# First attention: a new table of work-bank tasks, the value product in halves, and two copies on other engines

## The chip, the cores and the metric

The kernel runs on one core of one Trainium2 chip. The metric is the device time of one execution in microseconds. TensorE (PE) does matrix products and transposes, VectorE (DVE), ScalarE (ACT) and GpSimd (POOL) the rest, SyncE (SP) issues DMAs. Each engine takes its instructions in order; they wait for each other by semaphores.

## The reference, cut to what matters

Four layers in a row, each followed by a layer norm of input plus output: an attention, a feed-forward of four small stages, a linear attention, and a feed-forward of six blocks. Only the first attention is changed. It has 4 batches of 512 rows of 256 numbers and 16 heads of 16:

```python
qkv = jnp.einsum('bsh,hf->bsf', hidden_states, w_qkv) + b_qkv
qkv = qkv.reshape(B, S, NUM_HEADS, 3 * HEAD_DIM)
# q, k, v per head; the first 4 of 16 dimensions of q and k are rotated
scores = jnp.einsum('bhqd,bhkd->bhqk', q, k)
causal = jnp.tril(jnp.ones((S, S), dtype=bool))
scores = jnp.where(causal, scores, jnp.float32(-jnp.inf).astype(scores.dtype))
probs = jax.nn.softmax(scores, axis=-1)
attn = jnp.einsum('bhqk,bhkd->bhqd', probs, v)
attn = jnp.transpose(attn, (0, 2, 1, 3)).reshape(B, S, H)
return jnp.einsum('bsh,hf->bsf', attn, w_out) + b_out
```

## The kernel before

`attention0` runs all four batches. An *entry* is one batch: `entry(0, "first")`, a loop over the two middle ones (`"loop"`), `entry(3, "last")`. An entry has 8 *pairs* p of heads, a pair has 4 *slots* r, one for each tile of 128 rows; (p, r) names a slot. Every engine has its own `entry` that walks the same 32 slots, so the order on each engine is written out by hand.

In a slot TensorE does `max_pass` for the pair after next (two products q x k into banks 0 and 1, from which VectorE's `maximum` takes the row maxima), in slot 1 `max_rows` (a transpose of the negated maxima into the exchange bank; VectorE's `take_rows` copies it out and a DMA puts it into `qT`), a piece of the `value_pass`, the `score_pass` (two products k x q into one of the banks 2 to 4), and at most one task of the *work bank*. ScalarE's `exponentials` make `probs` from the scores, GpSimd's `select` zeroes what lies behind the diagonal. `J_ORDER` gives the tile that a slot works on: 512, 128, 384 and 256 columns in slots 0 to 3. The value product of a group q (two pairs, four heads) is done in the four slots of pair 2q + 2, one piece in each, before the slot's scores. Then ScalarE's `copy_outputs` (slot 3 of that pair) moves the sums out of bank 6, and in slot 2 of the next odd pair `transpose_outputs` puts them through the exchange bank, from where VectorE's `take_outputs` divides them.

The work bank (PSUM bank 5) holds one task at a time; the next may begin when the reader of the last has read it. The tasks, from the tables `UNIT_AT`, `PREVIOUS` and `AHEAD`:
- `project` (half of the heads u, tile t): six products make q, k and v of one tile and 8 heads; VectorE's `take_work` adds the bias into `qkv`. Then GpSimd's `rotate` (four instructions), ScalarE's `stack_high` (two: the parts of q and k rounded to fp32r), VectorE's `stack_low` (two subtractions: the rest).
- `stack`: four transposes of `k_stack` into the work bank, four of `q_stack` into the exchange bank. VectorE copies the first to `kT` (line 1028), ScalarE the second to `qT` (`copy_q`, line 759).
- `x_T`, `att_T`, `next_T` (c = 0, 1): four transposes of the next batch's input, the finished attention or the finished norm of the batch before. ScalarE's `high` copies the rounded part, then VectorE's `low`, one slot later in its order, subtracts for the rest, and frees the bank.
- `out` (0, 1): twelve products with the output weights; VectorE adds the residual. Behind `out` 1 comes the layer norm, its steps spread over the slots from (4, 0) on.

In an entry the second half's four tiles are projected and stacked in pairs 0 to 2, the next batch's first half in pairs 4 to 6; `att_T`, `x_T` and `out` stand in (2, 2) to (3, 3), `next_T` in (6, 2) and (6, 3). Pair 7 has no task. The exchange bank (PSUM bank 7) is used in turn by `max_rows`, `stack` and `transpose_outputs`; its readers count up `ex_read`, those of the work bank `v_work`.

Before the first entry the weights are split and the first half of batch 0 is projected and stacked; after the last the value product of its last group and the last output are done. Then the next part of the kernel (`prep`) starts and fetches its weights.

## Time and profile before

| | us |
|---|---|
| median of 3 runs | 1283.71 |
| lowest, highest | 1275.53, 1283.94 |
| the profiled execution's own time | 1284.08 |
| its span, first to last instruction | 1282.4 |
| mean granted TensorE clock over the span | 0.899 |

The rows come from the profiled execution, with times in us from the start of its span. A granted clock of 1.00 in a stretch is 2.4 GHz throughout, 0.50 is 1.2 GHz throughout; nothing between is granted, so a mean tells the shares. The busy time of TensorE counts weight loads apart (PEld), which overlap the products. The first attention ends at about 385 us of the span.

### The profile page before, as it was taken

What the parts mean: (1) busy time and instruction counts of PE and PEld (TensorE: products, weight loads), DVE (VectorE), ACT (ScalarE), POOL (GpSimd) and SP (SyncE); (2) the same over time, 40 slices, a digit from 0 to 9 for tenths busy, and PEclk for the clock granted to TensorE, in tenths of its full rate; (3) what the DMA queues carried; (4) which work ended last, traced back from release to release, by engine and by line L of the source; (5) the groups of instructions that cost most, each with busy time, mean ns of one, the idle gap of its engine ahead of it and who ended that gap; (6) DMA issues with size and microseconds to landing.
All of it is one profiled execution on the core that took longest, in us unless ns stands there. A gap on an engine that the chain in (4) does not pass through costs nothing. (4 is left out here: it accounts for less than half of the span.)

```text
span 1282.4 us, 20711 instructions
## 1 busy us (share of the span) xinstructions
PE 1098.8 (86%) x6653; PEld 898.6 (70%) x6653; DVE 806.2 (63%) x2286; ACT 604.6 (47%) x1149; POOL 273.8 (21%) x361
## 2 busy tenths in 40 slices
PE   3789889889857667863886999999999999999996
PEld 3545455545435557863775898989989989989895
DVE  2666676577636257787357557666666676576664
ACT  2245534445422364534432746556466465564560
POOL 1223323134220230020001112312313214213200
PEclk9978887788778778975896999999999999999999
DMA  4000000000007100000001200101000000101110
GB/s 158 17 2 18 2 18 18 1 17 2 18 1 264 66 1 1 0 0 3 0 18 36 80 1 34 34 1 33 33 0 33 33 0 33 33 0 33 33 34 33
DMA packets 28589, 36.56 MB, mean 29 GB/s; under 512 B 1412, under 2 KB 25704, under 8 KB 28520
## 3 DMA queue, kind: packets, MB, share of 16 engines
q1 hardware_dynamic: 25912, 31.80, 7.4%
q10 hardware_dynamic: 2608, 3.93, 0.9%
q8 instruction: 33, 0.54, 0.2%
q14 instruction: 36, 0.29, 0.1%
HBM read 31.40 MB, written 4.19 MB: 28 GB/s over the span
## 5 line engine op out<-in xcount | busy, mean ns | idle before, releaser
L1825 ACT ACTIVATE G<-ps,bias_col 128x512 f32<-128x512 f32 x192 | 135.2, 704 | 188.8 <-PE ps L1743 177.5
L1758 PE MATMUL ps<-w_h,G_h 128*128 128x256 f32 x768 | 217.7, 283 | 1.4 <-DVE rsum L1886 1.4
L1758 PE MATMUL ps<-w_h,G_l 128*128 128x256 f32 x768 | 217.3, 283 | 0.0
L1758 PE MATMUL ps<-w_l,G_h 128*128 128x256 f32 x768 | 217.1, 283 | 0.0
L1877 DVE TENSOR_TENSOR G_l<-G,G_h 128x512 fp32r<-128x512 f32 x192 | 136.2, 719 | 62.9 <-ACT G_h L1826 62.8
L766 ACT ACTIVATE probs<-ps 128x512 f32<-128x512 f32 (+3 forms) x256 | 97.4, 436 | 148.5 <-PE ps L829 148.4
L1743 PE MATMUL ps<-xT_h,w_h 128*128 128x512 f32 x384 | 154.2, 401 | 1.7 <-PEq L1358 1.7
L1743 PE MATMUL ps<-xT_l,w_h 128*128 128x512 f32 x384 | 152.8, 398 | 0.0
L1743 PE MATMUL ps<-xT_h,w_l 128*128 128x512 f32 x384 | 152.6, 397 | 0.0
L1705 POOL TENSOR_TENSOR x_a<-xn,mlp_g 128x1024 f32<-128x1024 f32 x20 | 72.1, 3606 | 368.4 <-DVE xn L1909 368.4
L967 DVE CUSTOM_DVE_ANT_0 ps<-ps,q_mask 128x128 f32<-128x128 f32 (+3 forms) x256 | 121.5, 512 | 46.3 <-PE ps L818 39.6
L1758 PEld LDWEIGHTS ps<-w_h,G_h 128*128 128x128 f32 x768 | 147.2, 192 | 2.4 <-issue 1.6
L1758 PEld LDWEIGHTS ps<-w_l,G_h 128*128 128x128 f32 x768 | 147.2, 192 | 0.8
L1758 PEld LDWEIGHTS ps<-w_h,G_l 128*128 128x128 f32 x768 | 147.2, 192 | 0.0
L1826 ACT ACTIVATE G_h<-ps,bias_col 128x512 fp32r<-128x512 f32 x192 | 134.7, 702 | 0.0
L1886 DVE TENSOR_TENSOR rsum<-ps,x_a 128x1024 f32<-128x1024 f32 x24 | 29.4, 1224 | 118.7 <-PE ps L1758 118.7
L680 POOL TENSOR_SCALAR_AFFINE_SELECT probs<-probs 128x256 f32<-128x256 f32 x128 | 52.0, 409 | 209.1 <-ACT probs L766 209.0
L818 PE MATMUL ps<-kT,qT 64*128 64x128 f32 (+3 forms) x256 | 77.5, 475 | 19.5 <-DVE top_score L967 18.9
L1743 PEld LDWEIGHTS ps<-xT_h,w_h 128*128 128x128 f32 x384 | 72.9, 190 | 18.5 <-issue 2.0
L1871 DVE TENSOR_TENSOR xT_l<-hs,xT_h 128x512 fp32r<-128x512 f32 x40 | 80.5, 2039 | 7.8 <-ACT xT_h L1813 7.7
L1743 PEld LDWEIGHTS ps<-xT_h,w_l 128*128 128x128 f32 x384 | 72.9, 190 | 17.4
L1743 PEld LDWEIGHTS ps<-xT_l,w_h 128*128 128x128 f32 x384 | 73.0, 190 | 16.6
(248 smaller groups left out, 2165.1 us busy)
## 6 DMA issues: line engine op xcount, KB each, us to landing
w_raw<-L_ffn_W_T SPq DMA_DIRECT2D x12, 1024.0 KB, 5.1
hs<-L_attn_hidden_states SPq DMA_DIRECT2D x8, 512.0 KB, 3.5
x_kept<-hs SPq DMA_DIRECT2D x4, 512.0 KB, 2.9
w_raw<-x_kept SPq DMA_DIRECT2D x2, 1024.0 KB, 5.9
out<-xn SPq DMA_DIRECT2D x4, 512.0 KB, 2.9
w_raw<-L_ffn_ent_w_T SPq DMA_DIRECT2D x1, 1024.0 KB, 10.5
w_raw<-L_ffn_ent_pw SPq DMA_DIRECT2D x1, 1024.0 KB, 12.6
qT<-neg_rows SPq DMA_DIRECT2D x64, 2.0 KB
```

The costliest lines, as they stand in the source:

```text
L680: pool.affine_select(diagonal, diagonal, [[0, 2], [1, P]], ALU.is_ge, 0.0, base=0, channel_multiplier=-1).then_inc(s["g_sel"], 1)
L766: act.activation(probs[:, p % 2, o, OFF[j]:OFF[j] + COLS[j]], ps[:, score_bank(r, o), 0:COLS[j]], ACT.Exp).then_inc(s["a_exp"], 1)
L818: pe.matmul(ps[:, o, 0:(t + 1) * P], qT[rows, p, t * P:(t + 1) * P], kT[rows, p, 0:(t + 1) * P], start=True, stop=True).then_inc(s["p_max" ...
L967: v.tensor_tensor_reduce(ps[:, o, 0:(t + 1) * P], ps[:, o, 0:(t + 1) * P], q_mask[:, S - (t + 1) * P:S], 1.0, MASKED, ALU.add, ALU.max, to ...
L1705: pool.tensor_tensor(g.x_a[:, rows, :], xn[:, b % 2, :, :], bcast(g.mlp_g[:, i, :], 1, [P, RT, D]), ALU.mult).then_inc(s["g_mul"], 1)
L1743: mm = pe.matmul(ps[:, n % 4, :], w[:, c, f * P:(f + 1) * P], x[:, b, c, :], start=(k == 0), stop=(k == 5))
L1758: mm = pe.matmul(ps[:, 4 + t // 2, (t % 2) * D:(t % 2 + 1) * D], x[:, b % 2, f, t * P:(t + 1) * P], w[:, f, :], start=(k == 0), stop=(k == ...
L1825: act.activation(G32[:, n % 4, :], ps[:, n % 4, :], ACT.Gelu, bias=bias)
L1826: act.activation(G_h[:, b % 2, f, :], ps[:, n % 4, :], ACT.Gelu, bias=bias).then_inc(s["a_g"], 1)
L1871: v.tensor_tensor(g.xT_l[:, b, c, :], src, g.xT_h[:, b, c, :].bitcast(F32), ALU.subtract).then_inc(s["v_T"], 1)
L1877: v.tensor_tensor(G_l[:, b % 2, f, :], G32[:, n % 4, :], G_h[:, b % 2, f, :].bitcast(F32), ALU.subtract).then_inc(s["v_gl"], 1)
L1886: v.tensor_tensor(g.rsum[:, :, :], ps[:, 4:6, :].rearrange("p a (b c) -> p (a b) c", c=D), g.x_a[:, b * RT:(b + 1) * RT, :], ALU.add).then ...
```

## The change

One table `WORK_AT` takes the place of three and spreads the tasks over all eight pairs. Heads are counted in halves: 1 is the second half of the batch, 2 and 3 are both halves of the next. The second half of the next batch is now projected in pairs 6 and 7 of the entry before it, and only stacked in its own; in the preparation its four projections stand between the first maxima. The slots of `stack_high` and of the low parts are given by `HIGH_AT` and `LOW_AT`. `stack_low` moves from VectorE to GpSimd, the copy of `kT` from VectorE to ScalarE (`copy_k`, ahead of `copy_q`). The scores stand before the value product in a slot; the value product of group q is done in slots 2 and 3 of pair 2q + 1 and slots 0 and 1 of pair 2q + 2; `copy_outputs` comes in slot 2, `transpose_outputs` and `take_outputs` in slot 3 of that same pair. `v_work` is renamed `work_read`, `v_stack` `g_stack`. The diff, cut:

```diff
-UNIT_AT = ((0, 0, "project", 0), (0, 2, "project", 1), (0, 3, "stack", 0), (1, 0, "project", 2),
-           (1, 1, "stack", 1), (1, 2, "project", 3), (1, 3, "stack", 2), (2, 1, "stack", 3))
-VALUES_AT = {(1, 0): (0, 1), (1, 1): (2,), (1, 3): (3,)}
-PREVIOUS = ((2, 2, "att_T", 0), (2, 3, "att_T", 1), (3, 2, "out", 0), (3, 3, "out", 1),
-            (6, 2, "next_T", 0), (6, 3, "next_T", 1))
-AHEAD = ((3, 0, "x_T", 0), (3, 1, "x_T", 1))
+
+
+WORK_AT = ((0, 0, "stack", (1, 0)), (0, 2, "stack", (1, 1)), (0, 3, "x_T", 0),
+           (1, 0, "stack", (1, 2)), (1, 1, "x_T", 1), (1, 3, "stack", (1, 3)),
+           (2, 0, "att_T", 0), (2, 1, "project", (2, 0)), (2, 2, "att_T", 1),
+           (3, 0, "out", 0), (3, 1, "project", (2, 1)), (3, 3, "out", 1),
+           (4, 0, "stack", (2, 0)), (4, 1, "project", (2, 2)), (4, 2, "stack", (2, 1)),
+           (5, 0, "project", (2, 3)), (5, 1, "stack", (2, 2)), (5, 3, "stack", (2, 3)),
+           (6, 0, "project", (3, 0)), (6, 1, "project", (3, 1)), (6, 2, "next_T", 0),
+           (7, 0, "project", (3, 2)), (7, 1, "next_T", 1), (7, 3, "project", (3, 3)))
+HIGH_AT = {(0, 0): (1, 1), (0, 2): (1, 2), (1, 1): (1, 3), (3, 2): (2, 0), (4, 0): (2, 1), (4, 3): (2, 2),
+           (5, 2): (2, 3), (7, 2): (3, 0)}
+LOW_AT = {(0, 1): (1, 1), (0, 3): (1, 2), (1, 2): (1, 3), (3, 3): (2, 0), (4, 1): (2, 1), (5, 0): (2, 2),
+          (5, 3): (2, 3), (7, 3): (3, 0)}
+VALUES_AT = {(0, 3): ((1, 0), (1, 1)), (1, 0): ((1, 2),), (1, 1): ((1, 3),),
+             (4, 3): ((2, 0), (2, 1)), (5, 0): ((2, 2),), (5, 2): ((2, 3),)}
+PREVIOUS = ("att_T", "out", "next_T")
+AFTER = [(kind, n) for kind in PREVIOUS for n in range(2)]
+BEFORE = [("project", (2, 0)), ("project", (2, 1)), ("stack", (2, 0)), ("project", (2, 2)),
+          ("stack", (2, 1)), ("project", (2, 3)), ("stack", (2, 2)), ("stack", (2, 3))]
+
+
+def of_entry(when, half):
+    return half == 1 or when != "last"
 
 
 def work_table(when):
 
-    rows = [(p, r, kind, (1, t)) for p, r, kind, t in UNIT_AT]
-    if when != "last":
-        rows += [(p + 4, r, kind, (0, t)) for p, r, kind, t in UNIT_AT] + list(AHEAD)
-    if when != "first":
-        rows += PREVIOUS
-    return {(p, r): (kind, arg) for p, r, kind, arg in sorted(rows, key=lambda row: row[:2])}
+    table = {}
+    for p, r, kind, arg in WORK_AT:
+        if kind in PREVIOUS:
+            used = when != "first"
+        else:
+            used = when != "last" if kind == "x_T" else of_entry(when, arg[0])
+        if used:
+            table[p, r] = (kind, arg)
+    return table
+
+
+def group_at(p, r, when):
+    return r == RT - 1 and p % 2 == 0 and (p > 0 or when != "first")
 
...
                 uses.append((kind, arg))
-            if r == 2 and p % 2 and (p > 1 or when != "first"):
-                uses.append(("group", (p - 3) // 2))
+            if group_at(p, r, when):
+                uses.append(("group", p // 2 - 1))
...
+            def stack_low(i, half, t):
+                pool.wait_ge(s["a_stack"], tile_number(i, half, t) + 1)
+                heads = qkv[:, t, :].rearrange("p (h c d) -> p h c d", h=UH, c=3)
+                pool.tensor_tensor(q_stack[:, :, DH:2 * DH], heads[:, :, 0, :],
+                                q_stack[:, :, 0:DH].bitcast(F32), ALU.subtract)
+                pool.tensor_tensor(k_stack[:, :, 2 * DH:3 * DH], heads[:, :, 1, :],
+                                k_stack[:, :, 0:DH].bitcast(F32), ALU.subtract).then_inc(s["g_stack"], 1)
...
+                        if (p, r) in LOW_AT and of_entry(when, LOW_AT[p, r][0]):
+                            stack_low(i, *LOW_AT[p, r])
                         select(i, p, r)
                         kind, arg = table.get((p, r), (None, None))
                         if kind == "project":
                             rotate(i, when, *arg)
-                        u = 1 if p < UP else 0
-                        if (p % UP, r) in VALUES_AT and (u or when != "last"):
-                            if (p % UP, r) == (1, 0):
-                                wait(pool, s["p_out"], i * GROUPS + (0 if u else GROUPS // 2))
-                                pool.sem_inc(g.carrier["g_carrier"], 1)
-                            for t in VALUES_AT[p % UP, r]:
-                                values(i, u, t)
+                        for half, t in VALUES_AT.get((p, r), ()):
+                            if of_entry(when, half):
+                                if t == 0:
+                                    wait(pool, s["p_out"], i * GROUPS + (half - 1) * GROUPS // 2)
+                                    pool.sem_inc(g.carrier["g_carrier"], 1)
...
             for t in range(RT):
-                rotate(-1, "before", 0, t)
-                values(-1, 0, t)
+                rotate(-1, "before", 2, t)
+                values(2, t)
+                stack_low(-1, 2, t)
+            for t in range(RT):
+                rotate(-1, "before", 3, t)
+            stack_low(-1, 3, 0)
...
+            def copy_k(i, when, half, t):
+                u = half % 2
+                act.wait_ge(s["p_work"], WORK.number(i, when, ("stack", (half, t))))
+                act.activation(kT[:, u * UP:(u + 1) * UP, t * P:(t + 1) * P],
+                               work.rearrange("p (b c) -> p b c", c=P), ACT.Copy).then_inc(s["work_read"], 1)
+
+            def copy_q(i, when, half, t):
+                u = half % 2
+                act.wait_ge(s["p_ex"], EXCHANGE.number(i, when, ("stack", (half, t))))
                 act.activation(qT[:, u * UP:(u + 1) * UP, t * P:(t + 1) * P],
                                exchange.rearrange("p (b c) -> p b c", c=P), ACT.Copy).then_inc(s["ex_read"], 1)
...
                         exponentials(i, p, r)
-                        if r == RT - 1 and p % 2 == 0 and (p or when != "first"):
+                        if r == 2 and p % 2 == 0 and (p or when != "first"):
                             copy_outputs(i, when, p // 2 - 1, ("neg", p + 1))
                         kind, arg = table.get((p, r), (None, None))
                         if kind == "stack":
+                            copy_k(i, when, *arg)
                             copy_q(i, when, *arg)
                         elif kind in ("x_T", "att_T", "next_T"):
                             high(i, when, kind, arg)
-                        if before[0] == "project":
-                            stack_high(i, *before[1])
-                        before = (kind, arg)
+                        if (p, r) in HIGH_AT and of_entry(when, HIGH_AT[p, r][0]):
...
-                        if p and p % 2 == 0:
-                            value_pass(i, p // 2 - 1, r)
-                        elif p == 0 and when != "first":
-                            value_pass(i - 1, GROUPS - 1, r)
                         score_pass(i, p, r)
+
+                        if p % 2 and r >= 2:
+                            value_pass(i, p // 2, r - 2)
+                        elif p % 2 == 0 and r < 2 and p:
+                            value_pass(i, p // 2 - 1, r + 2)
+                        elif p == 0 and r < 2 and when != "first":
+                            value_pass(i - 1, GROUPS - 1, r + 2)
                         if (p, r) in table:
                             use_work(i, when, *table[p, r])
-                        if r == 2 and p % 2 and (p > 1 or when != "first"):
-                            transpose_outputs(i, when, (p - 3) // 2)
+                        if group_at(p, r, when):
+                            transpose_outputs(i, when, p // 2 - 1)
...
-            for _, _, kind, t in UNIT_AT:
-                use_work(-1, "before", kind, (0, t))
+            for kind, arg in BEFORE:
+                use_work(-1, "before", kind, arg)
             for p in range(2):
                 for t in range(RT):
                     max_pass(0, p, t, (-1, "before"))
+                    if p == 0:
+                        use_work(-1, "before", "project", (3, t))
                     if p and t == 1:
                         max_rows(-1, "before", 0, 0)
             entries(pe, entry)
-            for r in range(RT):
+            for r in range(2, RT):
                 value_pass(B - 1, GROUPS - 1, r)
             transpose_outputs(B - 1, "after", GROUPS - 1)
-            for _, _, kind, arg in PREVIOUS:
+            for kind, arg in AFTER:
                 use_work(B, "after", kind, arg)
 
...
-            def stack_low(i, u, t):
-                v.wait_ge(s["a_stack"], tile_number(i, u, t) + 1)
-                heads = qkv[:, t, :].rearrange("p (h c d) -> p h c d", h=UH, c=3)
-                v.tensor_tensor(q_stack[:, :, DH:2 * DH], heads[:, :, 0, :],
-                                q_stack[:, :, 0:DH].bitcast(F32), ALU.subtract)
-                v.tensor_tensor(k_stack[:, :, 2 * DH:3 * DH], heads[:, :, 1, :],
-                                k_stack[:, :, 0:DH].bitcast(F32), ALU.subtract).then_inc(s["v_stack"], 1)
 
...
-                elif kind == "stack":
-                    u, t = arg
-                    v.tensor_copy(kT[:, u * UP:(u + 1) * UP, t * P:(t + 1) * P],
-                                  work.rearrange("p (b c) -> p b c", c=P)).then_inc(s["v_work"], 1)
...
-                    kind, arg = table.get(slots[n - 2], (None, None)) if n >= 2 else (None, None)
-                    if kind == "project":
-                        stack_low(i, *arg)
                     kind, arg = table.get((p, r), (None, None))
-                    if kind in ("project", "stack", "out"):
+                    if kind in ("project", "out"):
                         take_work(i, when, kind, arg)
-                    if r == 2 and p % 2 and (p > 1 or when != "first"):
-                        take_outputs(i, when, (p - 3) // 2)
```

## Rows read from the trace of the kernel before

**Rows 1.** The page: busy time by engine, the clock by slices, two groups of section 5.
```profile
span 1282.4 us, 20711 instructions
...
PE 1098.8 (86%) x6653; PEld 898.6 (70%) x6653; DVE 806.2 (63%) x2286; ACT 604.6 (47%) x1149; POOL 273.8 (21%) x361
...
PEclk9978887788778778975896999999999999999999
...
L766 ACT ACTIVATE probs<-ps 128x512 f32<-128x512 f32 (+3 forms) x256 | 97.4, 436 | 148.5 <-PE ps L829 148.4
...
L818 PE MATMUL ps<-kT,qT 64*128 64x128 f32 (+3 forms) x256 | 77.5, 475 | 19.5 <-DVE top_score L967 18.9
```
**Rows 2.** Windows: busy us (instructions) by engine; clock; preparation, four entries, tail.
```profile
0.00:52.16 52.16, 24.94 (x84) 17.49 (x84) 20.48 (x60) 9.42 (x17) 8.60 (x26) 1.00 0.30 101
52.16:124.62 72.46, 66.25 (x373) 39.03 (x373) 49.54 (x189) 35.87 (x93) 22.77 (x72) 0.85 0.05 13
124.62:208.22 83.60, 70.68 (x445) 43.32 (x442) 56.49 (x209) 38.83 (x98) 25.91 (x74) 0.85 0.04 14
208.22:296.83 88.61, 75.73 (x444) 46.01 (x441) 57.92 (x217) 38.62 (x98) 25.94 (x74) 0.77 0.02 7
296.83:361.00 64.17, 58.20 (x353) 33.20 (x349) 40.39 (x156) 32.36 (x82) 18.32 (x52) 0.79 0.03 10
361.00:385.00 24.00, 12.51 (x74) 7.76 (x72) 8.50 (x28) 2.53 (x6) 3.83 (x4) 0.71 0.00 1
```
**Rows 3.** Windows of the second entry, same columns: about pair 2, pair 3, pair 7.
```profile
141.00:151.50 10.50, 8.44 (x71) 4.30 (x71) 7.70 (x28) 5.94 (x16) 2.51 (x7) 1.00 0.01 4
151.50:167.20 15.70, 11.76 (x65) 8.13 (x65) 8.34 (x29) 4.75 (x11) 1.64 (x4) 0.67 0.01 1
...
199.10:208.20 9.10, 7.66 (x31) 3.54 (x31) 5.55 (x21) 3.55 (x9) 4.84 (x6) 0.62 0.18 61
```
**Rows 4.** Timeline of the second entry, x_T 0 and 1 in the work bank.
```profile
153.15 0.84 PE L898 MATMUL ps<-ident,hs 128*128 128x128 f32 x4 [1.19 <-DVE att_l L1004]
...
154.02 0.60 ACT L741 ACTIVATE x_h<-ps 128x512 fp32r<-128x512 f32 x1 [0.94 <-PE ps L898]
...
155.62 0.67 DVE L1004 TENSOR_TENSOR x_l<-ps,x_h 128x512 fp32r<-128x512 f32 x1
...
156.34 1.12 PE L898 MATMUL ps<-ident,hs 128*128 128x128 f32 x4 [1.14 <-DVE x_l L1004]
```
**Rows 5.** Timeline of the second entry, the norm's statistics and TensorE's next product.
```profile
169.59 1.40 DVE L95 BATCH_NORM_STATS2 ln_stats<-rsum 128x6 f32<-128x256 f32 x4
...
172.37 0.82 PE L818 MATMUL ps<-kT,qT 64*128 64x384 f32 x2 [2.33 <-DVE top_score L967]
```
**Rows 6.** Groups by line and shape, 44 to 362 us; the number before the second bar: mean ns.
```profile
L1028 DVE CAST kT<-ps 128x512 fp32r<-128x512 f32 x28 | 19.1, 683 | 1.4 <-PE ps L876 1.4
...
L759 ACT ACTIVATE qT<-ps 128x512 fp32r<-128x512 f32 x28 | 16.8, 602 | 13.2 <-PE ps L903 13.2
...
L754 ACT ACTIVATE k_stack<-qkv 128x256 fp32r<-128x256 f32 x28 | 11.6, 413 | 0.0
...
L1013 DVE TENSOR_TENSOR k_stack<-qkv,k_stack 128x128 fp32r<-128x128 f32 x28 | 7.9, 283 | 0.0
```
**Rows 7.** Groups of GpSimd by line and shape, the whole span.
```profile
L691 POOL TENSOR_TENSOR hs<-hs,b_out 128x1024 f32<-128x1024 f32 x4 | 9.4, 2358 | 0.0
L665 POOL TENSOR_TENSOR turned<-qkv,rope 128x64 f32<-128x64 f32 x32 | 9.4, 294 | 47.2 <-DVE qkv L1024 47.0
...
L672 POOL COPY val<-qkv 128x128 f32<-128x128 f32 x32 | 9.0, 293 | 0.0
```
**Rows 8.** Timeline of the preparation: a projection's reader, a stack, the first maxima.
```profile
28.50 0.56 DVE L1024 TENSOR_TENSOR qkv<-ps,b_qkv 128x384 f32<-128x384 f32 x1 [2.38 <-PE ps L869]
...
34.79 0.72 PE L876 MATMUL ps<-ident_r,k_stack 128*128 128x128 f32 x4 [1.26 <-DVE k_stack L1013]
...
39.54 0.47 PE L818 MATMUL ps<-kT,qT 64*128 64x128 f32 x2
```

More of the change, by code:

```diff
@@ L512, in number @@
         return (i - 1) * len(self.lists["loop"]) + start + self.lists[when].index(key) + 1
-WORK = Uses([("x_T", 0), ("x_T", 1)] + [(kind, (0, t)) for _, _, kind, t in UNIT_AT],
-            lambda when: list(work_table(when).values()), [row[2:] for row in PREVIOUS])
-EXCHANGE = Uses([("stack", (0, t)) for t in range(RT)] + [("neg", 0)], exchange_list, [("group", -1)])
+WORK = Uses([("x_T", 0), ("x_T", 1)] + BEFORE + [("project", (3, t)) for t in range(RT)],
+            lambda when: list(work_table(when).values()), AFTER)
+EXCHANGE = Uses([("stack", (2, t)) for t in range(RT)] + [("neg", 0)], exchange_list, [("group", -1)])
 def attention0(nc, A, g):
@@ L776, in entry @@
                 table = work_table(when)
-                before = (None, None)
                 for p in range(PAIRS):
@@ L794, in _ @@
             for t in range(RT):
-                stack_high(-1, 0, t)
-                copy_q(-1, "before", 0, t)
+                stack_high(-1, 2, t)
+                copy_k(-1, "before", 2, t)
+                copy_q(-1, "before", 2, t)
+            stack_high(-1, 3, 0)
             entries(act, entry)
@@ L1089, in _ @@
                             ALU.subtract).then_inc(s["wsplit_l"], 1)
-            for n, (_, _, kind, t) in enumerate(UNIT_AT):
-                if kind == "stack":
-                    stack_low(-1, 0, t)
-                take_work(-1, "before", kind, (0, t))
+            for kind, arg in BEFORE:
+                if kind == "project":
+                    take_work(-1, "before", kind, arg)
             for p in range(2):
@@ L1096, in _ @@
                     maximum(0, p, t)
+                    if p == 0:
+                        take_work(-1, "before", "project", (3, t))
                     if p and t == 1:
```

57 lines of the change are left out of this document (30 added, 27 removed).

## Prediction

> **What bounds the kernel now.** I read the page first. TensorE is busy 86% of the span, the other engines 63% or less, and the row of granted clock sinks to 5 to 8 tenths in the first third of the span [rows 1]. The chain that ended last cannot be followed back past 703 us, so for the stage that is changed I read the windows by stage instead. The four entries of the batch loop last 72.46, 83.60, 88.61 and 64.17 us; before them lie 52.16 us of preparation, after them 24 us of tail [rows 2]. In the entries TensorE is busy 270.86 of 308.84 us, 88%, while VectorE has about 66%, ScalarE under 50%, GpSimd 30%. TensorE is nearly the bound, and two things make it long. It stands idle for 308.84 - 270.86 = 38.0 us. And its clock is below full: a granted mean c means that a share 2(1 - c) of the stretch ran at 1.2 GHz, which is 0.30, 0.30, 0.46 and 0.42 of the four entries, 21.7 + 25.1 + 40.8 + 27.0 = 114.6 us. What is busy there would take half the time at 2.4 GHz: 114.6 x 0.88 / 2 = 50 us. So entries with the same work would need about 308.8 - 38.0 - 50 = 221 us if nothing waited and the clock stayed up. The gain to be had is large, and most of it is clock.
>
> Next I asked where the clock falls. The stretch of pair 2, stacks, transposes and value product together, keeps 2.4 GHz although TensorE is idle for 2 of its 10.5 us; pair 3, with no value product, has 0.67; pair 7, with no task and no value product, 0.62 [rows 3]. The lulls are where the work is thin. In pair 3 the timeline shows why TensorE also stands still: transposes into the work bank (0.84 us), ScalarE copies the high part (0.60), VectorE, behind its maxima, makes the low part (0.67), and only then may TensorE use the bank again, after 1.14 us idle [rows 4]. In a middle entry five uses of the bank stand behind such a user in the very next slot (att_T twice, x_T twice, next_T once): about 5 x 1.3 = 6.5 us. A different wait is the layer norm: its statistics keep VectorE for 1.40 us and hold the next maximum, TensorE waits 2.33 us [rows 5].
>
> **The change, part by part.** *The clock.* The tables move no work out of an entry as a whole (the loop still has 16 project and stack tasks and 8 others), but the projections, before in pairs 0, 1, 4 and 5, now stand in pairs 2 to 7, and each value product is cut in two halves, slots 2 and 3 of the odd pair and slots 0 and 1 of the next even one. No pair is left without a value product, and pairs 3 and 7, the thin ones of [rows 3], get projections. What is left thin is pairs 0 and 1, which lose theirs and hold four stacks and two transposes; pair 2 of before, of that sort, kept its clock, the start of pair 3 did not, so I let each entry keep about 12 us at 1.2 GHz, the length of those two pairs less their value halves: 48 us instead of 114.6. Gain (114.6 - 48) x 0.88 / 2 = 29 us. Bounds: nothing at all if the lulls only move, and 42 us if 5 us are left in each entry.
>
> *The bank's chain.* Of the five adjacent uses of a middle entry two remain (x_T 0 before a stack, att_T 0 before a project): 3 x 1.3 = 3.9 us less, twice. The last entry loses all its three, 3.9 us; the first has one before and after. Sum 12 us.
>
> *VectorE.* It loses per full entry 8 copies of kT at 0.683 us and 16 subtractions at 0.285 [rows 6]: 5.5 + 4.6 = 10 us of some 57 busy. It is not the bound, so only its waits count: TensorE's score products of the maxima waited 18.9 us for it in all [rows 1], of which some 7 belong to the norm, that stays. I take 5 of the rest as gained; ends 0 and 12.
>
> *ScalarE.* It gets the kT copy, at the price of its neighbour qT, 0.602 us [rows 6]: 8 x 0.60 = 4.8 us an entry onto 38.8 busy. Before, VectorE copied kT while ScalarE copied qT. Now one engine does exponentials, kT, qT, and in three slots the two stack_high copies of 0.41 as well. Behind qT waits the exchange bank. After the new tables max_rows (slot 1) comes right after the stacks of (0,0), (1,0) and (4,0), and transpose_outputs right after that of (4,2), which on ScalarE also stands behind copy_outputs. From the end of the k transposes the copies need 0.60 + 0.60, and TensorE has about 0.35 us of other work to cover them: 0.85 us idle, three times; for (4,2) 1.2 us. That is 3.75 us in three entries, 1.7 in the last, and 2 in all for the kT copy that holds the work bank where the exponentials come late: 15 us more. Ends: 7 (ScalarE is early) and 56 (below).
>
> *GpSimd.* No row shows its subtraction of 128x128. From 128x64 at 0.294 us and 128x1024 at 2.358 [rows 7] the slope is 2.15 ns an element, so 0.43 us, two of them 0.87 a tile instead of VectorE's 0.57. Ends 0.29 (its own copy of that size, one input) and 0.6. Per entry 7 us on an engine with 26 busy; HIGH_AT and LOW_AT leave at least one slot of about 2 us for it before the transposes. Only from (4,0) to (4,2) is the chain full (kT, qT, two stack_high, two subtractions, 2.9 us, against some 3.5 us of TensorE's work), so I cost it at nothing; without that cover it would be 0.3 us a tile, 9 us in all. The Trainium skill speaks against this part: GPSIMD Engine Reference, § 4.1, gives two-input elementwise work to VectorE, as GpSimd is about 2x slower there. By it a tile costs twice 0.57, 1.14 us, an estimate 0.27 us over mine and still under the cover, so the sum would be the same; the page's rule counts an engine's time, and here GpSimd's time is idle. The rows for the same work (0.43 extrapolated against 0.285) say 1.5x.
>
> *Scores before values.* The exponentials start sooner by one piece of the value product; ScalarE is not the bound, I cost it at nothing. The value product needs select two slots back instead of four: two exponentials of 0.44 us on average [rows 1] and select end inside one slot.
>
> *Preparation.* Four projections (3, t) come into it, one behind each max_pass of pair 0, from 39.54 us on, where VectorE set the pace. Each is 2.38 us there, with VectorE waiting [rows 8]; half is hidden: +4 us. The low parts no longer stand behind the next take_work on VectorE (1.26 us of TensorE's wait in each tile, [rows 8]), about 0.7 us sooner in three tiles: -2. The same four leave the last entry; that is inside its shares. *Tail.* Two of four value passes leave the 24 us tail: -2.
>
> Sum: -29 (clock) - 12 - 5 + 15 (idle, together -2) + 4 - 2 - 2 = -31 us. The stage's end moves everything behind it, since the next weights are fetched when it ends. The profiled execution took 1284.08 us (span 1282.4), 0.4 over the median of 1283.71: 1284 - 31 = 1253.
>
> **The rivals.** *More than that:* the clock stays up everywhere but 5 us an entry (-42) and new waits are 7 instead of 15 (-8 more): 1253 - 13 - 8 = 1232. For it: pair 2 of before at 1.00. Against it: thin pairs 0 and 1.
>
> *The lulls only move:* the new waits and thin pairs 0 and 1 take back what pairs 3 and 7 give; 114.6 us stay at 1.2 GHz. Then only idle and ends count: 1284 - 2 = 1282, no change. For it: pair 3 of before fell to 1.2 GHz with gaps of little over 1 us [rows 3, 4].
>
> *ScalarE becomes the bound, slower:* each of the 28 stack slots in the entries shows its whole chain of 0.60 + 0.60 + 0.82 = 2.0 us on TensorE: 56 us instead of 15, that is 1253 + 41 = 1294. Place: max_rows and transpose_outputs behind the stack. It decides from 31 / 28 = 1.1 us a stack more than I took. Against it: pairs 0 and 1, the densest for ScalarE, ask of it 16 exponentials at 0.436 us [rows 1], four stacks at 1.20, three stack_high at 0.82, two x_T and one out_T at 0.60: 16.1 us, while two pairs of a middle entry take 20.9.
>
> **How the numbers follow.** The forecast 0.52 (own range 1240 to 1266), more 0.22, lulls only move 0.16, ScalarE bound 0.08, the rest anything. Over 1% is what a measurement of this kernel can tell from no change, 12.8 us, so below 1271 is faster: 0.52 + 0.22 + 0.03 = 0.77; 0.14 same; 0.09 slower. The range takes in the larger gain and most of the case without change: 1228 to 1284, leaving out some 0.17.
>
> **What would show it.** Right: the clock of the entries at 0.90 or more on average, with the rest of the low clock in pairs 0 and 1; pair 3 near 12 us instead of 15.7; idle of the entries near 35 us; TensorE's wait for VectorE's maxima shorter; a new wait of max_rows and transpose_outputs for ScalarE's qT of about 0.85 us; GpSimd's subtraction at 0.4 to 0.5 us with nobody waiting. Wrong: a clock at 0.81 or less as before; ScalarE leading the releasers of TensorE's waits with over 40 us; GpSimd's low parts released late to the k transposes.

## The result and the profile after

| | before | after |
|---|---|---|
| median, us | 1282.4 | 1241.26 |
| lowest, highest | 1275.53, 1283.94 | 1239.62, 1246.83 |
| span of the profiled execution | 1282.4 | 1237.7 |
| end of the first attention in the span | 387.4 | 349.3 |

The medians are 41.1 us apart. The ratio, which goes by all runs of both kernels, is 0.9702, 95% interval 0.9666 to 0.9737: about 38 us of 1280. The profiled execution of the changed kernel is the fastest of its four and has the highest granted clock of them, 0.927 over the span against 0.916 to 0.920. The page of the changed kernel, the rows that answer to [rows 1]:

```profile
span 1237.7 us, 20729 instructions
...
PE 1068.4 (86%) x6653; PEld 876.2 (71%) x6653; DVE 773.8 (63%) x2190; ACT 619.8 (50%) x1181; POOL 300.8 (24%) x425
...
PEclk9879999998787889858998999999999999999998
...
L812 ACT ACTIVATE probs<-ps 128x512 f32<-128x512 f32 (+3 forms) x256 | 98.2, 437 | 113.0 <-PE ps L877 112.3
...
L866 PE MATMUL ps<-kT,qT 64*128 64x128 f32 (+3 forms) x256 | 78.3, 457 | 12.5 <-DVE top_score L1019 12.0
```

TensorE has the same 86% and the same 6653 products, in 30 us less of busy time. The windows by stage show where, as [rows 2] did: preparation, four entries, the start of the tail; columns as there.

```profile
0.00:54.48 54.48, 31.06 (x108) 22.89 (x108) 16.98 (x52) 12.19 (x23) 16.77 (x52) 0.96 0.29 98
54.48:123.03 68.55, 61.49 (x382) 36.52 (x383) 40.91 (x160) 40.00 (x101) 28.45 (x84) 0.83 0.03 10
123.03:193.84 70.81, 64.54 (x442) 38.05 (x442) 49.55 (x190) 42.66 (x106) 30.96 (x87) 0.95 0.05 17
193.84:266.74 72.90, 65.12 (x443) 38.65 (x444) 50.04 (x190) 42.78 (x106) 32.59 (x91) 0.95 0.04 11
266.74:324.00 57.26, 50.21 (x325) 26.09 (x325) 36.50 (x146) 33.61 (x84) 19.80 (x51) 0.85 0.04 11
324.00:350.00 26.00, 12.47 (x74) 8.18 (x70) 8.77 (x28) 3.64 (x7) 3.40 (x3) 0.70 0.00 0
```

Read them as the prediction read [rows 2]. The entries last 269.52 us instead of 308.84, 39.3 less. TensorE is idle for 269.52 - 241.36 = 28.2 us instead of 38.0. At 1.2 GHz it ran for 0.34 x 68.55 + 0.10 x 70.81 + 0.10 x 72.90 + 0.30 x 57.26 = 54.9 us. The view gives 114.6 us for before, but that is too little: its record of the clock begins only at 61.3 us of the span, and the view counts what is not recorded as full clock. The same product takes 0.52 us before that point and 0.34 behind it:

```profile
59.70 0.52 PE L869 MATMUL ps<-wqkv_h,x_l 128*128 128x384 f32 x1
...
64.12 0.34 PE L869 MATMUL ps<-wqkv_h,x_l 128*128 128x384 f32 x1
```

So the 9.1 us from 52.16 to 61.3 were at 1.2 GHz as well, which makes 123.7 us. The kernel e8 below, the same up to there, has this stretch on record at 0.50 and needs the same 10.54 us for pair 0 of the first entry. The preparation's 1.00 in [rows 2] and its 0.96 here are too high for the same reason; the record of the changed kernel begins at 47.0, so its entries are complete. With the busy share of 0.90 the low clock cost 24.6 us; before, with 0.877, it cost 54.2. So the 39.3 us are 29.7 of clock and 9.8 of idle time, and nothing is left over. Around them: the preparation is 2.3 us longer (54.48 against 52.16), the tail, up to the last transposes of the attention, 1.1 shorter (from 324.00 to 349.3 against 361.00 to 387.4). Together 38.1 us.

The rest of the span is 888.4 us after the attention, 895.0 in the profile of before. These 6.6 us are not the change's: the twelve variants below have 886.6 to 892.7 us there, among them e4, e7 and e8, which keep the old table (888.7, 890.0, 889.5).

Pairs 3 and 7 of the second entry, the thin ones of [rows 3]:

```profile
149.93:158.72 8.79, 8.79 (x64) 5.93 (x66) 6.31 (x24) 3.67 (x10) 3.44 (x11) 1.00 0.01 2
...
186.42:193.84 7.42, 7.42 (x50) 4.59 (x52) 6.34 (x24) 4.16 (x11) 5.07 (x10) 1.00 0.14 44
```

Pair 3 took 15.64 us slot by slot and takes 8.79, pair 7 9.08 and 7.42, without a moment of idle time and at full clock. What stood still where is in TensorE's waits in the entries (total us, times, longest): first before, 52 to 361 us of its span,

```profile
PE ps L818 <- DVE top_score L967: 15.3, 32, 2.3
PE ps L898 <- DVE att_l L1004: 6.3, 5, 1.3
PE ps L898 <- DVE x_l L1004: 3.7, 3, 1.4
PE ps L903 <- DVE neg_rows L981: 3.5, 7, 0.9
PE ps L883 <- DVE x_l L1004: 3.2, 2, 1.6
PE ps L898 <- DVE xT_l L1004: 3.2, 3, 1.3
```

then after, 54 to 324 us:

```profile
PE ps L866 <- DVE top_score L1019: 10.3, 25, 1.8
PE ps L900 <- ACT qT L805: 5.0, 10, 0.6
PE ps L923 <- DVE x_l L1056: 2.9, 3, 1.1
...
PE ps L917 <- DVE att_l L1056: 1.6, 2, 0.8
PE ps L906 <- ACT qT L805: 1.4, 2, 0.7
PE ps L950 <- DVE neg_rows L1033: 1.3, 3, 0.5
...
PE ps L923 <- POOL k_stack L714: 0.7, 2, 0.5
```

The bank's chain (att_l, x_l, xT_l) went from 16.4 to 4.5 us, the maxima from 15.3 to 10.3, and the new waits for ScalarE's qT are 6.4 us.

### The profile page after: what moved, and what is told of

It reads as the page before. It is cut to its first block and busy times, and to the rows that moved or that the text cites. A ratio compares the mean times of both kernels' runs of the same rounds, so it can differ in the third digit from the quotient of the medians.

```text
span 1237.7 us, 20729 instructions
## 1 busy us (share of the span) xinstructions
PE 1068.4 (86%) x6653; PEld 876.2 (71%) x6653; DVE 773.8 (63%) x2190; ACT 619.8 (50%) x1181; POOL 300.8 (24%) x425
## 5 line engine op out<-in xcount | busy, mean ns | idle before, releaser
L812 ACT ACTIVATE probs<-ps 128x512 f32<-128x512 f32 (+3 forms) x256 | 98.2, 437 | 113.0 <-PE ps L877 112.3
L866 PEld LDWEIGHTS ps<-kT,qT 64*128 64x128 f32 x256 | 37.3, 204 | 63.1 <-DVE top_score L1019 45.8
```

Of the source, the lines that this page charges most:

```text
L812: act.activation(probs[:, p % 2, o, OFF[j]:OFF[j] + COLS[j]], ps[:, score_bank(r, o), 0:COLS[j]], ACT.Exp).then_inc(s["a_exp"], 1)
L866: pe.matmul(ps[:, o, 0:(t + 1) * P], qT[rows, p, t * P:(t + 1) * P], kT[rows, p, 0:(t + 1) * P], start=True, stop=True).then_inc(s["p_max" ...
```

## The experiments

The prediction put most of the gain on the filling of thin pairs, by the table and by the halves of the value product, and nothing on the order of scores and values. The rival theory is a chain: scores, exponentials, the rounded parts of a stack (ScalarE), its low parts, then the stack's transposes on TensorE. By it, what makes the chain late makes TensorE stand still for a microsecond, and the clock falls soon after; then every part of the change that shortens the chain is worth more than its own time. The table has all kernels that ran. Ratios are to before, run beside each variant on the same chip, with medians of 1280.34 us (e3 to e6), 1279.56 (e7 to e10) and 1277.29 (e1, e2, e11, e12); so compare the ratios, not the medians.

Idle and low clock are us of the four entries, from windows as above; for before, e4 and e7 the first 9.1, 9.7 and 9.8 us, which are not on record, are counted as low. The last column counts TensorE's standstills of over 1.0 us that begin at full clock in the entries. These three columns come from one profiled execution each, and executions differ: the mean granted clock of 57 executions of before was 0.885 to 0.910, and the two middle entries of the one profiled, with the same instructions, had 25.1 and 40.8 us of low clock. A difference of some 15 us in that column can be chance.

| kernel | median us | ratio, interval | idle | low clock | over 1.0 |
|---|---|---|---|---|---|
| before | 1282.4 | 1 | 38.0 | 123.7 | 10 |
| after | 1241.26 | 0.9702, 0.9666 to 0.9737 | 28.2 | 54.9 | 3 |
| e4 before + both engine moves | 1275.66 | 0.9977, 0.9942 to 1.0012 | 37.9 | 126.9 | 9 |
| e7 before + halves behind the scores | 1280.14 | 1.0006, 0.9974 to 1.0038 | 37.6 | 123.9 | 8 |
| e8 before + scores twice, pairs 3, 7 | 1277.54 | 1.0003, 0.9964 to 1.0043 | 35.0 | 99.1 | 10 |
| e3 after, both engine moves undone | 1256.88 | 0.9827, 0.9764 to 0.9890 | 30.7 | 85.1 | 5 |
| e1 after, low parts on VectorE | 1251.76 | 0.9827, 0.9781 to 0.9873 | 31.0 | 82.2 | 5 |
| e2 after, kT copy on VectorE | 1248.51 | 0.9781, 0.9758 to 0.9803 | 25.1 | 75.2 | 2 |
| e5 after, values before scores | 1269.89 | 0.9919, 0.9890 to 0.9949 | 32.6 | 101.1 | 9 |
| e11 the same, only in one slot | 1269.64 | 0.9949, 0.9918 to 0.9980 | 33.5 | 97.2 | 4 |
| e6 after, values whole | 1272.92 | 0.9940, 0.9898 to 0.9983 | | | |
| e9 after + scores twice, pairs 1, 5 | 1244.02 | 0.9728, 0.9679 to 0.9777 | 24.6 | 59.8 | 1 |
| e10 after + fuller preparation | 1244.71 | 0.9722, 0.9674 to 0.9769 | 26.3 | 75.7 | |
| e12 after, another table | 1254.74 | 0.9843, 0.9805 to 0.9881 | 29.9 | 69.1 | 3 |

**e3, the table and the order without the engine moves.**

```diff
-            def stack_low(i, half, t):
-                pool.wait_ge(s["a_stack"], tile_number(i, half, t) + 1)
...
-                            copy_k(i, when, *arg)
...
+            def stack_low(i, half, t):
+                v.wait_ge(s["a_stack"], tile_number(i, half, t) + 1)
...
+                elif kind == "stack":
+                    half, t = arg
+                    u = half % 2
+                    v.tensor_copy(kT[:, u * UP:(u + 1) * UP, t * P:(t + 1) * P],
+                                  work.rearrange("p (b c) -> p b c", c=P)).then_inc(s["work_read"], 1)
```

> The changed kernel with VectorE again copying kT and making the low parts of the stacked heads; task table, halves of the value product and their order stay. Theory A (the gain is the even work on TensorE, which keeps its clock and breaks up the bank's chain; the engines matter little): about 1248 us, 7 over the changed kernel's 1241, entries' clock at 0.90 or more. Theory B (the gain is the 10 us of VectorE's work an entry that others took over): about 1275, with TensorE waiting for VectorE's maxima as before, 18 us or more.

1256.88 us: the table, halves and order are worth 22 us (0.0173 of 1280), the engine moves 16 more on top of them (7 to 25 with both intervals). Neither guess had come near: the time lies between 1248 and 1275, and TensorE waits 11.4 us for the maxima, not 18.

**e4, the engine moves alone, on the kernel before.** The same functions on ScalarE and GpSimd, in the slots that before has.

> The kernel before with only the engines changed: ScalarE copies kT, GpSimd makes the low parts; old tables, whole value product. Theory A: 1275 to 1285 us, entries' clock near 0.81 as before. Theory B: 1255 or less.

Nothing that can be told from no change; the profile has the same idle time and low clock as before, and a preparation 2.4 us shorter. So the two moves are worth 3 us (at most 7) on the old table and 16 on the new one. A price for them alone does not exist.

**e7, the halves behind the scores, on the kernel before.** The edit cuts the value product in halves and also puts the scores before it, so it tests the two together. It also takes the one-slot shift of copy, transposes and division that goes with them.

```diff
-                        if p and p % 2 == 0:
-                            value_pass(i, p // 2 - 1, r)
...
                         score_pass(i, p, r)
+                        if p % 2 and r >= 2:
+                            value_pass(i, p // 2, r - 2)
+                        elif p % 2 == 0 and r < 2 and p:
+                            value_pass(i, p // 2 - 1, r + 2)
```

> The kernel before (old task tables, old engines) with only the value product in two halves behind the scores, its copy and transposes one slot earlier. Theory A (what counts is how evenly TensorE is loaded, slot by slot): pairs 3 and 7 are no longer without a value product, their granted clock rises from 0.67 and 0.62, and the time falls by 10 to 20 us to 1260 to 1270. Theory B (the task table alone did it): within 5 us of the kernel before.

No change. Pair 3 of the second entry goes from 15.6 to 13.8 us, but the low clock of the entries stays, 123.9 against 123.7 us: in the middle entries there is less of it in pairs 0 and 3 and more in pairs 4 and 5. Giving the thin pairs half a value product, with the scores first, is worth nothing on the old table and the old engines.

**e8, more work in the thin pairs, on the kernel before.** Every score product of pairs 3 and 7 is done twice, into the same place.

```diff
+                    for n in range(2 if p in (3, 7) else 1):
+                        mm = pe.matmul(ps[:, score_bank(r, o), 0:COLS[j]], kT[rows, p, j * P:(j + 1) * P],
+                                       qT[rows, p, j * P:S], start=True, stop=True)
+                    mm.then_inc(s["p_score"], 1)
```

> The kernel before with both score products of every slot of pairs 3 and 7 done twice (the second writes the same result): 1.2 us more TensorE work a pair, 9.6 us in all, and no wait changed. Theory A (the clock falls in these pairs because TensorE has little to do in them, and that costs more than waits): granted clock there well above 0.67 and 0.62, time no longer than before, 1270 to 1283, in spite of the added work. Theory C (the clock falls because of the gaps): clock as before, time up by 5 to 10 us, 1286 to 1292.

The 9.6 us that were expected to be added are too much. By the rows a doubled slot at full clock lasts 0.11 to 0.30 us longer, which makes 5 to 7 us in all. The interval of the ratio reaches from 5 us less to 5.5 us more, so whether the added work cost anything is open. In the profile the pairs 3 and 7 have 36.5 us of low clock instead of 59.4, as the first theory had it, while pairs 0 and 1 of the first entry have 21.3 instead of 9.1, where the edit changes nothing. So thin stretches seem to matter, but filling them brought no gain. The standstills stay at 10.

**e5, the order undone, on the kernel after.**

```diff
-                        score_pass(i, p, r)
-
                         if p % 2 and r >= 2:
                             value_pass(i, p // 2, r - 2)
...
+                        score_pass(i, p, r)
```

> The changed kernel with the piece of the value product before the scores in each slot, as in the kernel before. As costed in the prediction (the order is worth nothing, ScalarE is not the bound): within 3 us of 1241. Rival (ScalarE, which now copies kT too, is starved by scores that come late): 1250 or more, with ScalarE's idle before the exponentials longer than in the changed kernel.

This costs 28 us (22 to 34 with both intervals), more than any other part taken out of the changed kernel, by an edit that changes no instruction, only which comes first. My costing at nothing was wrong and the rival right: over the span ScalarE waits 135.6 us for the scores instead of 112.3. The timeline of the changed kernel in slot (5, 2) of the second entry, from the max products on (start, duration, engine, what):

```profile
172.64 0.44 PE L866 MATMUL ps<-kT,qT 64*128 64x384 f32 x2
...
172.92 0.34 PE L877 MATMUL ps<-qT,kT 64*128 64x384 f32 x2
173.19 1.90 PE L890 MATMUL ps<-probs,val 128*32 128x512 f32 x8
173.29 0.87 ACT L812 ACTIVATE probs<-ps 128x384 f32<-128x384 f32 x2
...
174.36 0.42 ACT L793 ACTIVATE k_stack<-qkv 128x256 fp32r<-128x256 f32 x1
...
175.35 0.46 POOL L714 TENSOR_TENSOR k_stack<-qkv,k_stack 128x128 fp32r<-128x128 f32 x1
...
176.54 0.58 PE L923 MATMUL ps<-ident_r,k_stack 128*128 128x128 f32 x4
```

and of e5, the same slot:

```profile
179.66 0.44 PE L866 MATMUL ps<-kT,qT 64*128 64x384 f32 x2
...
180.03 1.07 PE L890 MATMUL ps<-probs,val 128*32 128x512 f32 x8
...
181.03 0.44 PE L877 MATMUL ps<-qT,kT 64*128 64x384 f32 x2
...
181.50 0.87 ACT L812 ACTIVATE probs<-ps 128x384 f32<-128x384 f32 x2 [1.14 <-PE ps L877]
...
182.56 0.42 ACT L793 ACTIVATE k_stack<-qkv 128x256 fp32r<-128x256 f32 x1
...
183.56 0.45 POOL L714 TENSOR_TENSOR k_stack<-qkv,k_stack 128x128 fp32r<-128x128 f32 x1
...
184.07 0.54 PE L923 MATMUL ps<-ident_r,k_stack 128*128 128x128 f32 x4 [1.13 <-POOL k_stack L714]
```

Counted from the max products, the scores begin at 0.28 us after, at 1.37 in e5; the exponentials at 0.65 and 1.84; the low part ends at 3.17 and 4.35. The whole chain is 1.2 us later, about the value piece's length (1.07 us), and TensorE stands 1.13 us before the stack. This pair of rows is no clean comparison, though. The changed kernel runs the slot at 1.2 GHz, where the same piece takes 1.90 us and covers more of the chain. And the low clock in these two pairs is equal: the changed kernel has 3.4 us of it in pair 5, e5 has 3.4 us in pair 6. Only in the third entry does e5 have more, 17.0 us against 3.4.

**e11, the order undone in one slot only.** This tells whether that place carries the loss.

```diff
+                        if p % 2 and r == 2:
+                            value_pass(i, p // 2, 0)
                         score_pass(i, p, r)
...
-                        if p % 2 and r >= 2:
+                        if p % 2 and r == 3:
```

> The changed kernel, but at the third slot of an odd pair, where the value piece is two 256-column halves long (512 columns), the piece stands before the score matmuls again; at the fourth slot it stays behind them. If the 28.6 us that the piece before the scores cost came mainly from this one place (late scores, late exponentials, a stack that waits over 1 us at (5,3), then low clock in pair 6), then most of it is lost here too: 1258 to 1270 us, the stack at (5,3) waits over 1 us, the low clock of the four entries adds up to over 85 us. If the loss was spread over both slots of every odd pair, about half of it or less: 1248 to 1256 us, low clock 60 to 80 us.

All of the loss is there: ratio 0.9949, e5 0.9919, the intervals overlap. The stack at (5, 3) of the first entry gives the clean comparison, at full clock in both; first the changed kernel, then e11:

```profile
106.38 0.51 PE L923 MATMUL ps<-ident_r,k_stack 128*128 128x128 f32 x4 [0.52 <-POOL k_stack L714]
```

```profile
108.33 0.51 PE L923 MATMUL ps<-ident_r,k_stack 128*128 128x128 f32 x4 [1.37 <-POOL k_stack L714]
```

In e11 the clock falls 0.5 us later, and pairs 6 and 7 have 20.9 us of low clock; in the changed kernel they have none. In e5 the same stack waits 1.51 us, and no fall follows. The row at (5, 3) of e11's second entry and its windows of pairs 5 and 6:

```profile
192.97 0.54 PE L923 MATMUL ps<-ident_r,k_stack 128*128 128x128 f32 x4 [1.27 <-POOL k_stack L714]
```

```profile
182.73:193.96 11.23, 9.12 (x58) 4.87 (x58) 7.84 (x30) 5.16 (x14) 5.13 (x16) 0.85 0.01 3
193.96:204.19 10.23, 9.73 (x56) 5.67 (x56) 5.29 (x20) 4.60 (x12) 3.54 (x12) 0.83 0.00 1
```

The changed kernel needs 9.55 and 8.76 us for these two pairs, at 0.82 and 1.00. With the longest piece of the value product in front (512 columns, slot 2 of the odd pairs) the scores are late where a stack hangs on them. The edit is in the third slot of all odd pairs; that the stack at (5, 3) alone carries the loss is not shown.

**e6, the value product in one pair.** On the kernel after: four pieces in the slots of the next even pair, before the scores, and copy_outputs, transpose_outputs and take_outputs where before had them.

> The changed kernel with each value product whole in the even pair, before the scores, as in the kernel before; task table and engines as changed. Theory A1 (the task table alone keeps TensorE's clock): within 6 us of 1241. Theory A2 (the halves are needed, since odd pairs without a value product are thin whatever their tasks): 1255 to 1265, with the granted clock below 0.8 in pairs 1, 5 and 7.

1272.92 us, by the ratio 0.9940 some 30 us over the changed kernel, near e5 and over both guesses. Halving the product gains nothing without the order: e5, halved and values first, is as slow. A whole product behind the scores was not tried. Only the times of e6 are used.

**e1 and e2, the engine moves one by one.** e1: stack_low as in the diff of e3; e2: the kT copy as there.

> The changed kernel, with the low parts of the stacked heads on VectorE again (the keys' copy stays with ScalarE). VectorE gets 10 tiles of 2 subtractions an entry back, 0.57 us a tile, and the stack no longer passes through GpSimd. If the 15.6 us that both moves give on top of the new table are VectorE's relief in proportion to the time taken from it (0.57 of about 1.4 us a tile), this loses about 6 us: 1247 us (1243 to 1252). If the chain ScalarE, then the low parts, then the stack decides, the faster engine for the low parts shortens it and the kernel is no slower than the changed one: 1238 to 1243 us.

> The changed kernel, with the copy of the transposed keys on VectorE again (the low parts stay on GpSimd). VectorE gets 10 copies an entry back, about 0.8 us each, in front of the transposed-query work and the row maxima; ScalarE gives up 0.60 us each. In proportion to VectorE's relief this loses about 9 us: 1250 us (1246 to 1256). If ScalarE's 0.60 us in front of an exponential cost as much as VectorE's copy did, there is no change: 1238 to 1244 us.

Against the changed kernel e1 loses 16 us (0.0125), e2 10 us (0.0079), and both together (e3) no more than e1. In proportion to VectorE's time I had expected 6 and 9: e2 is near it, e1 is not, and the other guess, that the faster engine shortens the chain, is wrong too. The timeline of e1 at (5, 2) and (5, 3) shows a wait that the faster engine brings:

```profile
181.85 0.42 ACT L783 ACTIVATE k_stack<-qkv 128x256 fp32r<-128x256 f32 x1
...
184.14 0.73 DVE L1009 CUSTOM_DVE_ANT_0 ps<-ps,q_mask 128x512 f32<-128x512 f32 x1
...
185.00 0.28 DVE L1055 TENSOR_TENSOR k_stack<-qkv,k_stack 128x128 fp32r<-128x128 f32 x1
...
185.34 0.55 PE L913 MATMUL ps<-ident_r,k_stack 128*128 128x128 f32 x4 [1.20 <-DVE k_stack L1055]
```

VectorE is faster at it (0.28 us) but gets to it behind the maxima: the low part ends 3.0 us after the rounded part, 185.28 - 182.27; on GpSimd (0.46 us) it ends 1.0 us after, 175.81 - 174.78. No fall of the clock follows this wait; in the first entry the same stack waits 1.34 us, the clock falls 1.4 us later, and pairs 6 and 7 have 13.6 us of low clock. In e2 the copy stands in the maxima's way instead, at (4, 2) and (4, 3):

```profile
161.05 0.69 DVE L1065 CAST kT<-ps 128x512 fp32r<-128x512 f32 x1
...
162.91 0.33 PE L858 MATMUL ps<-kT,qT 64*128 64x128 f32 x1 [0.46 <-DVE top_score L1011]
...
163.56 0.47 PE L858 MATMUL ps<-kT,qT 64*128 64x128 f32 x1 [0.33 <-DVE top_score L1011]
```

The clock falls right behind, and pair 5 takes 11.25 us instead of 9.55. These waits are short, and e2 as a whole stands idle for less than the changed kernel, 25.1 against 28.2 us: what it loses is clock, 75.2 us at 1.2 GHz against 54.9, and not behind a standstill of over 1.0 us here.

**e12, a table without the longest waits left.** The changed kernel still waits 1.12 us at (1, 0) (a stack behind the transposes of x at (0, 3); the expectation has 1.6) and 0.8 at (2, 1) (a projection behind those of the attention).

```diff
-           (1, 0, "stack", (1, 2)), (1, 1, "x_T", 1), (1, 3, "stack", (1, 3)),
-           (2, 0, "att_T", 0), (2, 1, "project", (2, 0)), (2, 2, "att_T", 1),
-           (3, 0, "out", 0), (3, 1, "project", (2, 1)), (3, 3, "out", 1),
+           (1, 1, "stack", (1, 2)), (1, 2, "x_T", 1),
+           (2, 0, "stack", (1, 3)), (2, 1, "att_T", 0), (2, 3, "att_T", 1),
+           (3, 0, "project", (2, 0)), (3, 1, "out", 0), (3, 2, "project", (2, 1)), (3, 3, "out", 1),
```

> The changed kernel with another table for its pairs 1 to 3: a stack or projection no longer comes in the slot right behind the transposes that feed it (before: transpose of x at (0,3), stack at (1,0), which waits 1.6 us for x's low part; transpose of attention at (2,0), projection at (2,1), which waits 0.8 us). If the waits are what is paid, the idle time falls by about 2 us an entry and some low clock goes with it: 1230 to 1237 us. If the waits only move to other slots (the projection now close behind the stack and the second transposes, the row maxima behind it), or the clock falls elsewhere, there is no gain: 1239 to 1246 us.

Eight tasks move, seven by one slot and one by three. 1254.74 us: 18 us slower than the changed kernel by the ratios (0.0141), outside both of my guesses. Pairs 1 and 2 did become shorter, 15.7 us together instead of 18.8. But the first task of pair 3 now follows att_T 1 directly, and the pair pays:

```profile
146.41 0.64 PE L917 MATMUL ps<-wqkv_h,x_h 128*128 128x384 f32 x1 [1.37 <-DVE att_l L1056]
```

```profile
144.52:158.40 13.88, 12.51 (x71) 9.07 (x72) 6.87 (x24) 3.67 (x10) 3.78 (x13) 0.75 0.01 2
```

13.88 us at 0.75 instead of 8.79 at 1.00: pair 3 of before is back, [rows 3]. The two middle entries together are 3.5 us longer than in the changed kernel and the last one 4.0, where low clock now covers pairs 5 to 7. That is 7.5 us; the profiled execution is with 1250.31 us the shortest of its kernel, and the rest of the 18 us it does not show.

**e9 and e10, can the rest of the low clock be filled?** e9 doubles the scores in pairs 1 and 5 of the changed kernel; e10 repeats max products in the preparation, so that TensorE is busier ahead of the first entry, which starts at 1.2 GHz.

> The changed kernel with the score products of pairs 1 and 5, where most of its remaining low clock lies, done twice: 9.6 us more work. Theory A: low clock in the entries falls from 56 us to 35 or less and the time stays within 5 us of 1241. Theory C: clock as in the changed kernel, time 1248 or more.

> The changed kernel with the maxima's products of the preparation (pairs 0 and 1 before the first entry) repeated 2 to 4 times, in time in which TensorE waits for VectorE. Theory A: TensorE comes into the first entry at 2.4 GHz instead of 20 us later, time 5 to 10 us less, 1232 to 1237. Theory C: no change, or 2 to 4 us more where the repeats are not hidden.

Neither is faster than the changed kernel, and neither clearly slower (0.9728 and 0.9722 against 0.9702, overlapping intervals). In e9 the low clock did not fall, 59.8 us against 54.9, so it is not the pattern of e8; the idle time is 3.6 us less. In e10 TensorE is busy for 13.3 of the 15.2 us before the first entry. Its clock is on record at 2.4 GHz from 42.3 to 52.6 us, falls 2 us before the entry begins and stays at 1.2 GHz for 20 us, as in the changed kernel: a fuller stretch ahead did not keep it.

## Why the prediction was right, and where it was not

The forecast was 1253 us, in a range from 1228 to 1284; the kernel takes 1241.26. The signs named in advance came near: the clock of the entries 0.90 on average, their idle time 28 us (35 expected), the low clock mostly in pairs 0 and 1 in the first entry, but in pairs 1 and 5 in the others. Against its own sum of -31 us stand -38.1 us in the stage. The time lies at the fast edge of the forecast's own range (1240 to 1266) and a little nearer to the rival's 1232 than to 1253.

- *The bank's chain, -12:* measured 16.4 - 4.5 = 11.9 us. *VectorE's maxima, -5:* 15.3 - 10.3 = 5.0. *Preparation +2, tail -2:* +2.3 and -1.1. These were right or near in size.
- *New waits, +15:* too much. The waits for qT are 6.4 us, longest 0.7, not 0.85 and 1.2 each; kT, out_T, the low parts on GpSimd and qkv add 3.4. Each of the first is real, but between the stack and the next user of the exchange bank TensorE now has the scores and the value piece to do. The wait for neg_rows fell by 2.2 besides. This one term is the 7 us by which the sum fell short.
- *GpSimd's subtraction, 0.43 us, at nothing:* the rows say 0.458 each, a tile 0.92, and in the entries the stack waits for it 0.7 us in all. In the preparation the stacks wait 3.1 us for the low parts, before 6.2.

```profile
L714 POOL TENSOR_TENSOR k_stack<-qkv,k_stack 128x128 fp32r<-128x128 f32 x27 | 12.4, 458 | 0.0
L712 POOL TENSOR_TENSOR q_stack<-qkv,q_stack 128x128 fp32r<-128x128 f32 x27 | 12.4, 458 | 16.1 <-ACT k_stack L793 15.9
```

- The rule that speaks against the move (the Trainium skill, GPSIMD Engine Reference, section 4.1: two-input elementwise work belongs to VectorE, about 2x faster there) has the direction right: 0.458 against 0.283 us [rows 6] is 1.6x. But e1 follows the rule and is 16 us slower; the low part then waits its turn behind the maxima.
- *The low clock, 114.6 to 48 us, -29:* measured 123.7 to 54.9 us and -29.7. I had read the unrecorded 9.1 us of the first entry as full clock. The size was right, the reason only in part, and that the two agree is in part luck: 12 us an entry were forecast, and 23.3, 7.1, 7.3 and 17.2 came, of which pairs 0 and 1 hold 30. I had said that pairs with value halves and projections keep the clock. e7 gives them the halves, with the scores first, and the low clock does not move; e5 has table, halves and engine moves and keeps 101 us of low clock. The forecast of pair 3 (near 12 us) was too high for the same reason: 8.79.
- *Scores before values, at nothing:* the step that failed. I priced it by ScalarE's load ("ScalarE is not the bound"), not by the chain that starts at the scores. It is worth 28 us with the rest in place (e5), all of it in one slot of the odd pairs (e11), and nothing, together with the halves, on the old table and engines (e7).
- *Work that leaves the entries:* no term, and none shows: clock and idle time account for the 39.3 us to within 0.2.

Of the rivals, "the lulls only move" is what happens when parts of the change are made alone (e4, e7), and "ScalarE becomes the bound" would have shown waits of 2 us behind each stack; the longest is 0.7. "More than that" asked for new waits of 7 us, and 9.8 came; but it also asked for 20 us of low clock, and 54.9 stayed, 23 of them in the first entry, the rest mostly in pairs 1 and 5 of the others.

So the gain is no sum of prices. On the old kernel, the engine moves are worth 3 us or so, halves and order together 0; table, order and halves together are worth 22, all together 38, and taking out the order costs 28, the low parts 16, the kT copy 10. The table alone was not run. The order shortens the way to a stack by 1.2 us, the low parts on GpSimd by 2.0. That these waits bring the 1.2 GHz behind them is the reading that fits most cases, not all.

**What stays open.** That the standstills cause the low clock is argued from their order in time, not shown by itself. In the profiles of before, after and ten of the variants (all but e6 and e10), 69 standstills of over 1.0 us began at full clock in the entries. For 59 of them the clock fell between their start and 4 us past their end (the limits are mine, for the count); of stretches as long, 5.3 us, laid anywhere at full clock, 26% meet a fall, so the two go together. But 10 had no fall, among them the stack at (5, 3) in both middle entries of e1, which waits 1.2 us; and of the 121 falls 65 had no such standstill just before. e8 suggests that the amount of work near the place matters too. What decides between a fall and none these runs do not tell.

## What to carry to other kernels

When an engine near its limit also has a clock that falls, price an edit by the chain that it moves, not by the load of the engine that it touches: ask which product releases the longest chain back to TensorE and issue that product first. In this kernel edits that moved that chain by 1 to 2 us each time it ran cost 16 to 28 us. The same order was worth nothing where the rest of the change was missing. Parts of such a change can be worth nothing alone and much together, so test them by taking one out of the whole, not only by putting one in; and a move to a slower engine pays if the faster one would only come to it later.

## What was not expected of the hardware

- Products that were added, 5 to 7 us of them in e8, made no difference that can be measured (ratio 1.0003, 0.9964 to 1.0043). In its profile the filled pairs had 36.5 us at 1.2 GHz instead of 59.4; in e9 the low clock did not fall.
- The same instructions had 25.1 us of low clock in one entry and 40.8 in the next (the middle entries of before).
- The first entry of the changed kernel starts at 1.2 GHz and stays there for 16 us, though TensorE is idle for only 0.3 us of the first pair. The clock had been at 2.4 GHz from 47.0 to 50.4 us and fell 4 us before the entry; making the preparation fuller (e10) did not change it.
- Eight tasks of one table, moved by one to three slots (e12), cost 18 us, more than the 4.5 us of waits that they were to remove in an execution.
